# An attention loop on one core: eight product chunks and exponentials three chunks wide, a head's copy moved from ScalarE to VectorE, scores issued eleven steps ahead

## The reference

```python
q = (x @ Wq.T).reshape(d, n, h)          # d = 128, n = 3327, h = 8
k = (x @ Wk.T).reshape(d, n, h)
v = (x @ Wv.T).reshape(d, n, h)
a = jnp.einsum('dnh,dmh->dnm', q, k) * scale
a = a + spatial_encoding + edge_encoding  # both are adj
a = jax.nn.softmax(a, axis=2)
out = jnp.einsum('dnm,dmh->dnh', a, v)
```

## Time and profile before

| | |
|---|---|
| profiled execution | 11756.2 us |
| its span | 11754.5 us (the execution is 1.7 us longer) |
| median of the three runs | 11779.06 us |
| PE busy | 10907.4 us, 93% |
| DVE busy | 10367.8 us, 88% |
| ACT busy | 10429.1 us, 89% |
| POOL busy | 6442.3 us, 55% |
| mean granted TensorE clock | 0.971 |

### The profile page before, as it was taken

How to read it: one execution, slowest core, us unless ns; L and a number is a source line. 1 busy time by engine, 2 the same in 40 slices (tenths; PEclk the granted TensorE clock), 3 DMA queues, 4 the chain that set the end, 5 groups by cost and what they waited for, 6 DMA issues and landing times. The chain is left out here.

```text
span 11754.5 us, 545122 instructions
## 1 busy us (share of the span) xinstructions
PE 10907.4 (93%) x216535; PEld 6944.7 (59%) x216535; DVE 10367.8 (88%) x10893; ACT 10429.1 (89%) x9224; POOL 6442.3 (55%) x3236
## 2 busy tenths in 40 slices
PE   8759999999999999999999999999999999999998
PEld 6525556555656556565655666656565566656566
DVE  7778988898988989888988898989888898988897
ACT  3359999999999999999999999999999999999996
POOL 4345555555555555555555555555555555555554
PEclk9889999999999999999999999999999999999999
DMA  6571111111121111111112111111112111111112
GB/s 223 179 232 39 39 39 39 39 39 39 39 69 44 39 39 39 39 39 38 40 39 75 39 39 39 39 39 39 39 36 77 39 39 37 40 38 38 39 39 81
DMA packets 573045, 653.23 MB, mean 56 GB/s; under 512 B 172173, under 2 KB 511251, under 8 KB 566867
## 3 DMA queue, kind: packets, MB, share of 16 engines
q1 hardware_dynamic: 570130, 617.66, 19.0%
q0 software_dynamic: 832, 1.71, 0.0%
HBM read 485.17 MB, written 133.77 MB: 53 GB/s over the span
## 5 line engine op out<-in xcount | busy, mean ns | idle before, releaser
L1074 DVE SCALAR_TENSOR_TENSOR at_double<-attention_adj_t,at_score 128x832 f32<-128x832 f32 x10240 | 9698.2, 1016 | 1127.8 <-PE at_score L1019 1121.9
L999 POOL TENSOR_TENSOR at_single<-at_single,attention_adj_t 128x832 f32<-128x832 f32 x3072 | 6106.0, 1988 | 4728.3 <-ACT at_single L1088 4695.6
L1091 ACT ACTIVATE at_double<-at_double 128x1664 f32<-128x1664 f32 x5120 | 8100.9, 1633 | 108.0 <-DVE at_double L1074 99.4
L1019 PE MATMUL at_score<-at_q,at_k 128*32 128x512 bf16 (+1 forms) x106496 | 7538.8, 353 | 450.8 <-ACT at_double L1091 383.9
L1035 PE MATMUL at_acc<-at_double,at_v 128*9 128x208 f32 x81920 | 5694.0, 344 | 151.2 <-issue 150.3
L1019 PEld LDWEIGHTS at_score<-at_q,at_k 128*32 128x32 bf16 x106496 | 3730.0, 145 | 2856.1 <-DVE at_double L1074 1126.9
L1088 ACT ACTIVATE at_single<-at_score 128x832 f32<-128x832 f32 x3072 | 2760.9, 899 | 657.9 <-PE at_score L1019 657.6
L1035 PEld LDWEIGHTS at_acc<-at_double,at_v 128*9 128x9 f32 x81920 | 2213.9, 92 | 1236.8 <-issue 255.0
L1035 PE MATMUL at_acc<-at_single,at_v 128*9 128x208 f32 x24576 | 1677.2, 341 | 0.0
L1035 PEld LDWEIGHTS at_acc<-at_single,at_v 128*9 128x9 f32 x24576 | 667.6, 92 | 292.3
L287 POOL TENSOR_TENSOR layer_col_acc<-layer_col_acc,st_a_rows 128x3328 f32<-128x3328 f32 x26 | 189.2, 7276 | 181.2 <-DMA st_a_rows<-in_adj_dram 181.2
(11 more groups left out here) (123 smaller groups left out, 1251.9 us busy)
## 6 DMA issues: line engine op xcount, KB each, us to landing
at_k<-k_parts_scratch SPq DMA_DIRECT2D x1536, 156.0 KB
at_q<-q_parts_scratch SPq DMA_DIRECT2D x4608, 13.0 KB
at_v<-v_scratch SPq DMA_DIRECT2D x512, 112.5 KB
adj_t_scratch<-st_a_t SPq DMA_DIRECT2D x26, 1664.0 KB, 7.6
st_a_rows<-in_adj_dram SPq DMA_DIRECT2D x25, 1663.5 KB, 8.8
attention_adj_t<-adj_t_scratch SPq DMA_DIRECT2D x16, 2080.0 KB, 16.5
attended_scratch<-at_o SPq DMA_DIRECT2D x1920, 7.3 KB
q_parts_scratch<-pr_partsq SPq DMA_DIRECT2D x39, 512.0 KB, 4.6
```

The costliest lines, as they stand in the source:

```text
L999: pool.tensor_tensor(slot(n), slot(n), at[:, plan.chunk[n], :], ALU.mult).then_inc(multiplied, 1)
L1019: last = pe.matmul(score[plan.buffer(n)][32 * t:32 * (t + 1), a:b], keys[:, 32 * t:32 * (t + 1)], q[k][:, a:b], start=True, stop=True, til ...
L1074: dve.scalar_tensor_tensor(out=slot(n), in0=at[:, plan.chunk[n], :], scalar=2.0, in1=score[plan.buffer(n)][:, 0:NB], op0=ALU.mult, op1=ALU ...
L1091: act.activation(doubles[buffer][:], doubles[buffer][:], ACT.Exp).then_inc(exped, 1)
```

## The change

`PRODUCTS` goes from 6 to 8, so 18 sum chunks are left. They are added into tiles of three chunks, `sum`, of which there are six, and one instruction of ACT exponentiates three chunks. `SCORE_LEAD` goes from 8 to 11. `keep_head` leaves ACT and becomes a DVE copy after the addition of step 14 of the next head. The number of `single` tiles stays 4 and the number of PSUM score buffers stays 3.

```diff
-DOUBLES = 8
+SUM_CHUNKS = 18
 SINGLES = 4
-PRODUCTS = 6
+PRODUCTS = 8
@@ class Steps
-        pairs = (C - products) // 2
-        self.doubles = next(k for k in range(DOUBLES, 0, -1) if GROUP * pairs % k == 0)
-        spread = sorted([((m + 0.5) / pairs, 2) for m in range(pairs)] + [((m + 0.5) / products, 1) for m in range(products)])
+        self.size = 3 if (C - products) % 3 == 0 else 2
+        sums = (C - products) // self.size
+        self.slots = next(k for k in range(SUM_CHUNKS // self.size, 0, -1) if GROUP * sums % k == 0)
+        spread = sorted([((m + 0.5) / sums, self.size) for m in range(sums)] + [((m + 0.5) / products, 1) for m in range(products)])
...
@@ attend
-        SCORE_LEAD = 8
-        KEEP_LAG = 5
+        SCORE_LEAD = 11
+        EXP_LEAD = 5
+        KEEP_AFTER = 14
...
@@ vector
+                def keep_head(i, b, head):
+                    k = head % 2
+                    dve.wait_ge(used, STEPS * i + (b * BODIES * STEPS + (head + 1) * C + AHEAD))
+                    dve.wait_ge(stored[k], STORES * (GROUP // 2) * i + STORES * (b * BODIES * (GROUP // 2) + head // 2 + 2))
+                    dve.tensor_copy(o[k][:], acc[k][:, 0:QW]).then_inc(kept, 1)
...
+                            if n % C == KEEP_AFTER:
+                                keep_head(i, b, n // C - 1)
@@ scalar
-                    act.activation(doubles[buffer][:], doubles[buffer][:], ACT.Exp).then_inc(exped, 1)
-            def keep_head(i, head):
...
-                act.activation(o[head % 2][:], acc[head % 2][:, 0:QW], ACT.Copy).then_inc(kept, 1)
...
+                    act.activation(sums[buffer][:], sums[buffer][:], ACT.Exp).then_inc(exped, 1)
+                with act.Fori(0, BLOCKS * BODIES) as i:
+                    for m in range(UNITS):
                         exponential(i, m)
```

More of the change, by code:

```diff
@@ L810, in __init__ @@
     def __init__(self, products):
-        pairs = (C - products) // 2
-        assert 2 * pairs + products == C
-        self.doubles = next(k for k in range(DOUBLES, 0, -1) if GROUP * pairs % k == 0)
-        spread = sorted([((m + 0.5) / pairs, 2) for m in range(pairs)] + [((m + 0.5) / products, 1) for m in range(products)])
+        self.size = 3 if (C - products) % 3 == 0 else 2
+        sums = (C - products) // self.size
+        assert self.size * sums + products == C
+        self.slots = next(k for k in range(SUM_CHUNKS // self.size, 0, -1) if GROUP * sums % k == 0)
+        spread = sorted([((m + 0.5) / sums, self.size) for m in range(sums)] + [((m + 0.5) / products, 1) for m in range(products)])
         self.n = GROUP * C
@@ L850, in slot @@
         same = [u for u, steps in enumerate(self.units) if (len(steps) == 1) == self.is_product[n]]
-        return self.is_product[n], same.index(self.unit[n]) % (SINGLES if self.is_product[n] else self.doubles), n - self.units[self.unit[n]][0]
+        return self.is_product[n], same.index(self.unit[n]) % (SINGLES if self.is_product[n] else self.slots), n - self.units[self.unit[n]][0]
     def last_like(self, what, n):
@@ L888, in attend @@
         plan = Steps(products)
-        doubles = [s.sb(f"double{k}", [P, 2, NB]) for k in range(plan.doubles)]
+        sums = [s.sb(f"sum{k}", [P, plan.size, NB]) for k in range(plan.slots)]
         singles = [s.sb(f"single{k}", [P, 1, NB]) for k in range(SINGLES if products else 0)]
@@ L922, in slot @@
             product, buffer, half = plan.slot(n)
-            return (singles if product else doubles)[buffer][:, half, :]
+            return (singles if product else sums)[buffer][:, half, :]
         def runs(eng):
@@ L958, in _ @@
                 for k in range(2):
-                    sp.sem_inc(stored[k], STORES)
+                    sp.sem_inc(stored[k], 2 * STORES)
                 sp.wait_ge(prefetched, 16 * len(Steps(PRODUCTS).prefetched))
@@ L983, in _ @@
                 for k in range(2):
-                    sp.wait_ge(stored[k], STORES * (BLOCKS * HEADS // 2 + 1))
+                    sp.wait_ge(stored[k], STORES * (BLOCKS * HEADS // 2 + 2))
         @block.gpsimd
@@ L1065, in _ @@
                     dve.memset(k_all[k][SHIFT_ROW:SHIFT_ROW + PARTS, 0:N], 1.0).then_inc(cleared, 1)
+                def keep_head(i, b, head):
[3 more added lines that the diff above has]
+                    dve.tensor_copy(o[k][:], acc[k][:, 0:QW]).then_inc(kept, 1)
+                dve.sem_inc(kept, 1)
                 for b in range(BLOCKS):
@@ L1075, in _ @@
                                                          in1=score[plan.buffer(n)][:, 0:NB], op0=ALU.mult, op1=ALU.add).then_inc(added, 1)
+                            if n % C == KEEP_AFTER:
+                                keep_head(i, b, n // C - 1)
+                keep_head(0, BLOCKS, -1)
         @block.scalar
@@ L1090, in exponential @@
                     act.wait_ge(added, plan.of_kind_before(i, steps[-1] + 1, False))
-                    act.activation(doubles[buffer][:], doubles[buffer][:], ACT.Exp).then_inc(exped, 1)
-            def keep_head(i, head):
-                act.wait_ge(used, STEPS * i + ((head + 1) * C + AHEAD))
-                act.wait_ge(stored[head % 2], STORES * (GROUP // 2) * i + STORES * (head // 2 + 1))
-                act.activation(o[head % 2][:], acc[head % 2][:, 0:QW], ACT.Copy).then_inc(kept, 1)
-            def body(i, more):
-                for m in range(KEEP_LAG, UNITS + KEEP_LAG):
-                    if m < UNITS or more:
-                        exponential(i, m)
[L1103 to L1112, removed]
+                    act.activation(sums[buffer][:], sums[buffer][:], ACT.Exp).then_inc(exped, 1)
+            with runs(act):
+                with act.Fori(0, BLOCKS * BODIES) as i:
+                    for m in range(UNITS):
+                        exponential(i, m)
 def project_out(nc, o_d, out, keep):
```

## The result

The changed kernel is slower: 13800.99 us (median of four runs, 13752.09 to 13857.85) against 11773.14 us of the kernel before in the same comparison. The ratio is 1.1735, with a 95% interval of 1.1669 to 1.1802. The forecast was 13350 us with a range of 12850 to 13950. So the direction and the range were right, and the centre was 451 us too low.

A forecast was written before the change was run, and what follows sets the result against it. ACT was taken as the bound inside a body, 19.53 us a pass. Passes +1725, body ends -141 and streaming +10 gave +1594 on 11756: 13350 us, range 12850 to 13950.

The forecast's parts named there:

- The new wait: ACT, second of two neighbouring products, twice a pass: 1.83 us wait, 3.9 us lost a pass; with other pass work +1725.
- The prices: Instruction times inside a pass: an ACT triple 2.18 us, the copy on DVE 0.36 us and hidden.
- Streaming: Before the attention, chunk stores and a third ACT exponential per column: +10 us, between 0 and 36.
- The end of a body: At PE's loop jump: 5.5 us lost a body instead of 6.6, from 3 to 9 possible; -141 us.
- the forecast's own case: Whole kernel slower, at 13000 to 13750 us; chance 75%.
- The second pause: PE after the jump: with the half clock it holds steps 13 and 17, 1.2 to 2.6 us more.
- The greater lead gives ACT nothing: SCORE_LEAD 11: three score buffers keep PE from running further ahead; its price is in the 1.83 us wait.
- The stall is not there: Rival: second products' scores are ready in time and ACT runs full; 11495 us, faster; chance 7%.
- The clock falls: Rival: PE's new pauses inside passes halve its clock; full case 15400 us, 8%, part case 13860, 7%.
- The part case: Clock rival with half clock in a quarter of the passes: 13860 us; chance 7%.

The follow-up runs named there:

- e3: Changed kernel with eight product tiles (SINGLES) instead of four; 13601.15 us, one run.
- e1: Changed kernel, but ACT takes the second of two neighbouring products before the triple in front of it; 12351.15 us, ratio 1.0522.
- e6: Kernel before with only the copy of a finished head moved from ACT to DVE; 11772.89 us, ratio 0.9996.
- e4: Changed kernel with ACT's loop rotated, the first five exponentials standing ahead of it; 13545.96 us, ratio 1.1524.
- e7: Kernel before with only SCORE_LEAD raised from 8 to 11; 11987.09 us, ratio 1.0222.
- e2: Changed kernel with SCORE_LEAD back at 8 instead of 11; 14055.61 us, one run.
- after: The changed kernel itself, against the kernel before; 13800.99 us, ratio 1.1735.
- e8: Changed kernel with second neighbouring products taken early, heads starting with a triple, eight product tiles and ACT's loop rotated; 11845.99 us, ratio 1.0068.
- e9: e8 with loop bodies of eight heads instead of four; 11423.48 us, ratio 0.9715 against the kernel before.
- e11: e8 with loop bodies of sixteen heads instead of four; 11051.80 us, ratio 0.9414 against the kernel before.

## Why the prediction was right, and where it was wrong

**The new wait: right.** The prediction built the round trip from links of the trace before, 0.05 + 0.76 + 0.35 + 0.53 + 0.14 = 1.83 us, and 2.69 from start to start. Measured: 1.77 and 2.64. The releaser, the two places in a pass and the order of the links are as forecast, e3 shows that the tile is the last link and that the scores alone would be 1.47, and e1 takes the stall away by the order alone. A pass came out at 22.83 us against 22.9; the term was 1725 and is 1690. e1 tested the order and e3 the tiles; the part of the three score buffers rests on PE's waits, since no run had a fourth.

**The prices: right.** A triple 2.18 (2.18), the copy 0.368 (0.36), and the copy is hidden in the changed kernel, where DVE is 70% busy. e6 shows how thin that cover is elsewhere: with six products the move gains nothing. Streaming was put at +10 and has no visible cost. One slip has no effect: 26 steps of PE at 0.71 us are 18.5 us, not 18.3.

**The end of a body: wrong.** The prediction put it at 5.5 us instead of 6.6, which is -141 us, and allowed 3 to 9. It is 9.7 us, outside these bounds, and +397: 538 us too low, more than the miss of the whole. The median, 13801, therefore also lies above the forecast's own case (13000 to 13750, 75%); the wider range of 12850 to 13950 held although this term had the wrong sign. Two things were left out.

- *The table load.* The prediction counted the exponentials and not what the start of the loop adds. It costs 1.43 us where it stands, and 2.0 us a body go with it when the loop is rotated (e4).
- *The second pause.* The prediction said that the scores of step 12 come 0.76 us after the first pause, at 8.2 us behind the exponential of step 4, and that the second pause holds only steps 13 and 17. By the timeline after, the second pause (2.42 us) stands before these scores, and the exponential of step 12 starts 11.9 us (5053.65 to 5065.51) after that of step 4 has ended. The order of the earlier trace rows, where two scores groups lie between the pauses, was carried over to a jump at another place. With that the second pause is also longer, 3.0 us on average against 1.25 before.

Without the table load 7.2 us are left in e4, 1.7 over the forecast. That e7 lost 2.0 us a body by the lead alone agrees with this reading, but in the old order of products. In the new order e2 has the lead of eight, and with its table loads still in place it loses 7.2 us at an end (bodies of 102.5 us, passes of 23.84) against 9.5: 2.4 less. Its passes have gaps of their own, so this supports the reading and doesn't isolate it.

**"The greater lead gives ACT nothing": right in the pass, wrong at the jump.** e7 leaves the pass as it is and costs 258 us.

**The rivals.** "The stall is not there" is out by the rows. "The clock falls" came true to a very small part: PE waits 1.9 us for ACT twice in a pass, and away from the jumps the clock went to half behind 21 of these waits, of some 770 in all. The part case of this rival, 13860 us, is nearer to the measured time than the forecast is, but by its number alone: it wanted a quarter of the passes and 512 us, and the 21 stretches are 72 us long together. The Trainium skill's rule on this in "TensorE: Matmul & The Clock Gate", section "A second HAM failure mode: psum-queue depth-cycling", has brief idle times between matmul groups swing the clock between its two levels. The trace agrees in those 21 places, and elsewhere inside the passes the clock stayed at 1.00. At the body's end the clock does fall, 0.70 over 5056 to 5065.5, with pauses of 3.40 and 2.42 us.

## What to carry to other kernels

Where an engine takes its work in a fixed order and k buffers feed it, look for places where two units of the kind that frees a buffer become neighbours: the second waits for a whole round trip, which can be summed from the links of the old trace to within 0.1 us, and moving one entry of the list can take it away. A loop's jump is a place of its own: every change of a lead or an order moves it, so it must be followed again instruction by instruction, with all that the compiler puts at the start of the body. If the loss at a jump grows little with the body's length, a longer body is the cheapest remedy: here it was 6.3 us with four heads and 8.3 with eight in the old kernel, and half the jumps brought 254 us.

## What the runs showed that was not expected

- PE stops twice at a jump of its loop, with nothing in the profile to wait for: 3.40 and 2.42 us after, 2.80 and 3.10 in e8, and the half clock follows. The second pause depends on where the jump stands: 1.25 us on average with scores eight steps ahead, 2.9 with eleven, and nothing else changed (e7).
- ACT reloads its table, 1.283 us, in every iteration when no activation stands ahead of the loop in its list, though all activations in the body are the same function (after, e1). With five ahead of it the load is gone (e4).
- The loss on ACT at a jump was 6.3 to 6.6 us at best and 8.8 to 10.7 in e8, e9 and e11, with no trend over bodies of 4, 8 and 16 heads.
- Idle times of PE of 1.9 us, twice in 22.8 us, mostly left the granted clock at 1.00, but not always: 21 times in after and 7 times in e4 it fell to half for 3.4 us in the middle of a body, and never in the kernel before and in e1, which have no such idle times there.
